# Sigmoid gates and scan rate in SBUF for all front steps of a vision tower, with the edge scans at other places

## The reference

```python
# tokenizer: gated 3x3 taps
t = unfold3x3(x)                                   # [B, 3136, 576]
h1 = relu(t @ W1 + b1);  s = sigmoid(h1 @ W2 + b2)
h = (t * s) @ W3 + b3
h = concat([cls_tok, h])                           # 3137 tokens per image
# state space: a linear two-component scan along the tokens
h = h + attn(layernorm(h))
# graph attention over the first 16384 nodes, 262144 random edges, self loops
e = leaky_relu(a_src[src] + a_dst[dst])
alpha = exp(e - segment_max(e, dst)) / segment_sum(...)
agg = segment_sum(h[src] * alpha, dst)
scores = layernorm(agg + b).mean(heads);  top-2 of 4 experts, softmax
out = h + sum_e gate_e * (gelu(x @ W1[e]) @ W2[e])
```

## Time and profile before

| what | us |
|---|---|
| median of 3 runs | 3913.06 (3908.71 to 3918.84) |
| the profiled execution | 3913.37 |
| its span, first to last instruction | 3911.4 |
| POOL busy | 2461.7 (63%) |
| DVE busy | 2237.5 (57%) |
| PE busy | 1957.8 (50%) |
| ACT busy | 1170.6 (30%) |

### The profile page before, as it was taken

One profiled execution on the slowest core, in us unless ns is written; L12 is line 12 of the kernel. 1 busy time (PEld: TensorE's weight loads), 2 busy tenths in 40 slices (PEclk: granted clock), 3 DMA queues, 4 the chain that ended last, 5 costly groups with the idle time before them and its releaser, 6 DMA issues. The chain is left out here.

```text
span 3911.4 us, 28658 instructions
## 1 busy us (share of the span) xinstructions
PE 1957.8 (50%) x7633; PEld 848.7 (22%) x7633; DVE 2237.5 (57%) x3952; ACT 1170.6 (30%) x1736; POOL 2461.7 (63%) x2477
## 2 busy tenths in 40 slices
PE   0451119988876868686765226776863300000034
PEld 0111114333322323232222102332331100000033
DVE  8889987887567676766767655555322020220355
ACT  0120004554443434343443124554563300000001
POOL 1000006776777777777777777777777777777573
PEclk9975558998888979898987568998986755555567
DMA  4110004544434444344432333333332311111134
GB/s 111 26 26 0 0 11 71 99 79 74 71 64 84 76 77 79 71 78 77 72 71 45 58 50 78 73 81 78 86 117 56 104 28 10 28 16 21 40 117 128
DMA packets 651925, 247.81 MB, mean 63 GB/s; under 512 B 552260, under 2 KB 632564, under 8 KB 649332
## 3 DMA queue, kind: packets, MB, share of 16 engines
q1 hardware_dynamic: 573844, 216.69, 23.7%
q0 software_dynamic: 77920, 29.29, 7.2%
HBM read 152.62 MB, written 91.71 MB: 62 GB/s over the span
## 5 line engine op out<-in xcount | busy, mean ns | idle before, releaser
L799 POOL DMA_INDIRECT ring<-table,src_i x2048 | 2017.4, 985 | 639.2 <-issue 525.7
L769 POOL DMA_INDIRECT ring<-keys_d,place x128 | 146.6, 1145 | 626.4 <-DVEq L1272 587.6
L1627 DVE TENSOR_TENSOR_SCAN early_i<-ns,cad,early_i 128x128 f32<-128x128 f32 (+2 forms) x68 | 26.4, 450 | 719.0 <-DMA ring<-table,src_i 719.0
L1006 PE MATMUL ps<-arena 64*128 64x512 f32 x800 | 218.4, 668 | 374.7 <-DMA arena<-xnT 252.2
L901 PE MATMUL ps<-arena,w 64*128 64x448 f32 x896 | 254.8, 648 | 185.6 <-DVE arena L1669 115.1
L1053 PE MATMUL ps<-ident,ends 128*20 128x128 f32 x6 | 1.5, 418 | 591.5 <-DVEq L1866 591.5
L1126 ACT ACTIVATE ex<-ex 128x1024 f32<-128x1024 f32 (+2 forms) x17 | 17.1, 1006 | 808.0 <-DVE ex L1642 808.0
L1203 ACT ACTIVATE arena<-ps,arena 128x1024 f32<-128x1024 f32 x200 | 212.7, 1115 | 116.8 <-PE ps L1006 116.7
L1669 DVE TENSOR_TENSOR arena<-arena,ps 128x448 f32<-128x448 f32 x297 | 172.3, 618 | 115.5 <-ACT ps L1120 115.3
L914 PE MATMUL ps<-arena,w 128*64 128x448 f32 x896 | 216.5, 606 | 39.2 <-issue 39.2
L1120 ACT ACTIVATE ps<-ps,tb 128x448 f32<-128x448 f32 x297 | 169.4, 604 | 210.7 <-PE ps L901 190.7
(11 more groups left out here) (346 smaller groups left out, 3940.1 us busy)
## 6 DMA issues: line engine op xcount, KB each, us to landing
arena<-in_x SPq DMA_DIRECT2D x304, 110.0 KB
ring<-table,src_i POOLq DMA_INDIRECT x2048
partial<-ring SPq DMA_DIRECT2D x15, 1536.0 KB, 6.1
arena<-in_x SPq DMA_DIRECT2D x160, 140.0 KB
outputs_d<-arena SPq DMA_DIRECT2D x32, 512.0 KB
arena<-outputs_d SPq DMA_DIRECT2D x32, 512.0 KB, 5.1
arena<-xnT SPq DMA_DIRECT2D x100, 128.0 KB, 3.1
arena<-h_tok SPq DMA_DIRECT2D x50, 256.0 KB
```

The source lines that it names most:

```text
L799: g.indirect_dma_start(out=ring[k % 2][:, j - FROM[k], :], out_offset=None, in_=table[0:GRAPH_NODES, :], in_offset=off(ap=src_i[:, j:j + 1 ...
L1006: m = mm(hid[ee % 2][:, z * NT:(z + 1) * NT], fw1[lower_upper(z), ee, :], xf[q][lower_upper(z), :], start=True, stop=True)
```

## The change

Three constants change. `PSUM_FROM` goes from 23 to 57, past the last step, so all 56 steps have the early form: ACT writes gates to SBUF, PE waits for `gate_done` where it waited for `prod_done`, the scans of the states read the rate from `par`, stand before and behind the ninth product, and the copy of the rate is gone. Seven scans behind turns become six, five behind pairs become four, and seven stand behind the pairs instead of five.

```diff
-PSUM_FROM = GRAPH_STEPS + 4
+PSUM_FROM = NSTEP + 1
 EARLY_STEPS = 17
-SCAN_AFTER_TURN = {31: 0, 37: 1, 43: 2, 49: 3, 54: 4, 59: 5, 63: 6}
-SCAN_AFTER_PAIR = {4: 7, 14: 8, 24: 9, 35: 10, 44: 11}
+SCAN_AFTER_TURN = {32: 0, 39: 1, 46: 2, 53: 3, 60: 4, 63: 5}
+SCAN_AFTER_PAIR = {2: 6, 15: 7, 30: 8, 44: 9}
```

## The result

The changed kernel takes 3980.26 us in the median of five runs (3974.47 to 3988.04), against 3908.71 for the kernel before beside it: a ratio of 1.0178, 95% interval 1.0163 to 1.0192. It is slower by 72 us, where 3980 us and 67 us more were forecast.

The account below looks back on a forecast made before the run. The prediction took POOL's back-to-back gathers as the bound: 3913.4 us plus 68 us (33 steps x (2.46 - 0.39)), less about 1 us, gives 3980 us. Its 8-in-10 range was 3935 to 4010 us.

Parts of the forecast that it names:

- The bound: POOL issues gathers one behind the other for 2669 us of the span; nothing else holds it.
- The price per step: Front steps 23 to 55: POOL loses 2.46 us a step in early form against 0.39 in late form.
- The early step with edge gathers (47 us): Lower alternative price from one early step, 1035.5 to 1057.1 us: gather mean 1050 ns, 1.8 us lost.
- The scatters (110 us): Upper alternative price from scatters in four early steps: mean 1207 ns, 3.7 us a step, 110 us at most.
- the sum: Whole kernel: 3913.4 us profiled plus 68 us on POOL, less about 1 us, gives 3980 us.
- The cause of the shorter step: Front steps: PE no longer waits for DVE's product; 21.2 against 27.3 us, 201 us off the front, costed at nothing.
- The reading of waits: POOL's gathers: no idle time put down to a store of DVE's results, so no gather waits for a ring half.
- The slack of the places: Moved edge scans: over 140 us of slack in the front, 36 us at the tightest, scan 9.
- No stall: Rival: gathers do not lengthen in converted steps; 3900 to 3913 us, chance 0.07.
- The front decides: Rival: gathers hang on the front's pace, so ending it 111 us earlier gives 3803 us; chance 0.05.
- The late half of the ring: Rival: a scan comes after its chunk's turn and POOL stands still; some 20 us on top, 4000 us, chance 0.04.
- The scatters' pattern: Rival: POOL settles at the longer stall pattern in converted steps, 3.7 us a step, 4023 us; chance 0.06.

Follow-up runs that it names:

- the form alone: Changed kernel with the edge scans at the places of the kernel before, so only the early form in all steps: 3981.1 us.
- the added products: Kernel before plus 120 DVE products ahead of each of scans 12, 13, 14: 3936.4 us with second input in SBUF, 3912.2 us with it in PSUM.
- the places alone: Kernel before with only the edge scans' new places, steps 23 to 55 keeping the late form: 4042.2 us.
- rate in SBUF alone: Kernel before with the four state scans of late steps reading their rate from SBUF, gates still in PSUM: 3946.4 us.
- scans' early place: Changed kernel with gates in PSUM in late steps; state scans before and behind the ninth product, rate from SBUF, new edge-scan places: 3922.6 us.
- 360 products with two SBUF inputs: Kernel before with 120 more DVE products ahead of each of scans 12, 13 and 14, both inputs in SBUF: 3936.4 us.

## Why the prediction was right, step by step

**The bound** held. POOL issues one gather behind the other in both kernels, the idle time between them is the same, and no speed of the front, of the experts or of their scans came through (the form alone ends the front 168 us later than the changed kernel does and takes the same time).

**The price per step** held to the digit in ordinary converted steps: 1108 ns, 15 gathers in 21.2 us. 33 x 2.07 = 68 us were forecast; the gathers' stretch grew by 70.7. The row with the same undisturbed duration and a settled step was the right one to take. The early step with edge gathers (47 us) was indeed not settled: the same step, which the change leaves alone, has 1100 ns in the trace after (1026.3 to 1047.9 us) and not 1050. The scatters (110 us) were too far.

That the sum came within 3 us is in part luck. It priced all 33 steps as ordinary ones, though some stand beside an edge scan or right behind one. The first 768 gathers, which run beside the front, after the change:

```profile
984.00:2070.30 1086.30, 836.09 (x768) 0.85 0.42 76
```

That is 77.6 us more than the 758.47 of the earlier trace rows, and not 68; the later gathers, 3 us shorter, and the idle time, 5.7 us less, made up for it.

**The mechanism** is shown and not only inferred: the added products change one operand's place and nothing else, and cost 22 us or nothing. The Trainium skill's remark against the sum (SBUF — State Buffer, section Who interferes with whom), that a probe saw `tensor_tensor` not stall DMAs whose descriptors GpSimd writes, does not hold for these gathers: `tensor_tensor` with two SBUF inputs lengthened them to 1070 ns. The other thing that the prediction took from there, that such an instruction contends with GpSimd's reads of SBUF, should not have counted against the sum: a gather takes its row numbers from `src_i`, which lies in SBUF, so by the Trainium skill's rule a stall was to be expected. No run here moves the row numbers elsewhere, so that it is this read that waits is not shown.

**The cause of the shorter step** was wrong in part. The prediction put all 6.1 us to PE, which waited for DVE's product. With the gates in SBUF and the scans left behind the inverse deviation, steps are 25 to 26 us at first and 27.2 later; the scans' place alone gives 24.2, and both 21.2. It cost nothing, since the step's length does not enter the sum.

**The reading of waits** was right for a weaker reason than given. That no idle time was put down to a store proved little: a wait of 52.9 us for a store stands under "issue" in the run with the places alone. What carries it is that the 1706 pieces before have a mean of 0.31 us and, more than that, how long the longest of them is. The row gives the sum, the number and the longest:

```profile
POOL ring L799 <- issue: 525.7, 1706, 1.8
```

With 1.8 us at the longest, no wait like the 52.9 us can hide there.

**The slack of the places** held. The last scan of the front started at 2071.7 us as worked out (2071), the front ended at 2095 (2094), the first gelu came at 2214 (2213). For scan 9 the bound was 36 us of slack; its exponential ran at 2805.6 us, its last instruction at 2821, and the gathers that need its half began at 2904.6. With 6 us for the store, the median from issue to landing, some 75 us were left.

**The rivals.** No stall fell with the rows of the steps. The front decides fell too: the front ended 110 us earlier and the time rose. The late half of the ring did not come about here, but the run with the places alone shows its size in long steps, 131 us. The scatters' pattern did not come about either.

## What to carry to other kernels

Find the engine whose queue never empties, and cost a change by what it does to that queue, even where the change touches other engines alone. On DVE an operand in PSUM can be worth more than a shorter step, if GpSimd's indirect DMAs are the path. Where the same code already runs in both forms somewhere in the trace, price the change from those stretches, and prefer the settled one with the same undisturbed duration.

## What the runs showed of the hardware that had not been expected

A gather that is held up ends a fixed time behind the DVE instruction in which it starts. In stretches of 30 to 80 us from five traces (before, the change, rate in SBUF alone, scans' early place, 360 products with two SBUF inputs) there are 43 gathers of over 1.03 us. Each starts inside a DVE instruction with two SBUF inputs, and each ends 0.75 to 0.76 us behind it if it is a scan and 0.80 to 0.82 us behind it if it is a product or another `tensor_tensor`. Six gathers in the same stretches start within 0.02 us of such an instruction's start, and keep their 0.94 to 0.95 us.

So the price is not one of the instruction but of where the gather starts in it. Four scans a step with two SBUF inputs left gathers at 967 ns in one order of DVE's instructions and at 993 ns in another. That may also be why the parts of the form, 36 us for the rate and 19 for the gates, fall short of its 70, but the whole form has another order and shorter steps as well, and no run separates these. What makes the starts of POOL and DVE settle in one pattern or the other was not tried.
